# Spreading GpSimd's indirect transfers: permutation scatters three per tile, single-word lookups fewer per half tile

## What is computed

```python
def gat_conv(x, src, dst, W, a_src, a_dst, bias):
    h = (x @ W).reshape(n, H, C)                       # H, C = 4, 256
    al_s = jnp.einsum('nhc,hc->nh', h, a_src)
    al_d = jnp.einsum('nhc,hc->nh', h, a_dst)
    e = jax.nn.leaky_relu(al_s[src] + al_d[dst], NEG_SLOPE)
    w = jnp.exp(e - segment_max(e, dst)[dst])
    alpha = w / segment_sum(w, dst)[dst]
    return segment_sum(h[src] * alpha[:, :, None], dst).reshape(n, H * C) + bias
h = relu(gat_conv(x, src, dst, W1, a_src1, a_dst1, b1))
h = relu(gat_conv(h, src, dst, W2, a_src2, a_dst2, b2))
x = layernorm(x + h @ Wfc + bfc)     # then three more layers on the edges
```

## Time and profile before

| | |
|---|---|
| timed runs | 2668.86 us median of 3 (2668.79 to 2675.23) |
| the profiled execution | 2661.8 us; span 2659.9 us |
| TensorE | 2356.0 us busy, 89%; granted clock 0.934 of full on average |
| weight loads | 1885.9 us, 71% |
| VectorE | 1527.7 us, 57% |
| ScalarE | 995.7 us, 37% |
| GpSimd | 1001.7 us, 38% |
| DMA | mean 148 GB/s |

### The profile page before, as it was taken

One profiled execution on the slowest core, in us unless ns is written; L12 is line 12 of the kernel. 1 busy time (PEld: TensorE's weight loads), 2 busy tenths in 40 slices (PEclk: granted clock), 3 DMA queues, 4 the chain that ended last, 5 costly groups with the idle time before them and its releaser, 6 DMA issues.

```text
span 2659.9 us, 33436 instructions
## 1 busy us (share of the span) xinstructions
PE 2356.0 (89%) x10787; PEld 1885.9 (71%) x10787; DVE 1527.7 (57%) x4649; ACT 995.7 (37%) x2005; POOL 1001.7 (38%) x971
## 2 busy tenths in 40 slices
PE   6977593696999998888989999999998987999997
PEld 4856482485788886766877888888886766777775
DVE  6746371474466683333433566378776765667754
ACT  4932010121126651111212566334433553555343
POOL 1052517302512226553052322135664544543532
PEclk8988796798999998988999999999999999999998
DMA  5323251354236752222222667456665655555432
GB/s 177 138 90 111 66 185 45 99 178 142 75 120 232 250 205 84 64 65 71 96 66 74 228 216 251 139 188 214 204 203 190 230 183 179 165 180 184 160 109 68
DMA packets 171539, 394.21 MB, mean 148 GB/s; under 512 B 44967, under 2 KB 73902, under 8 KB 170830
## 3 DMA queue, kind: packets, MB, share of 16 engines
q0 software_dynamic: 65296, 184.67, 22.4%
q1 hardware_dynamic: 106090, 207.66, 22.2%
HBM read 221.98 MB, written 170.25 MB: 147 GB/s over the span
## 4 chain that ended last, share of the span: by engine, by line
PE 61%; DVE 5%; issue 5%; ACT 2%; another core or an unknown queue 2%; DMA 1%; POOL 0%; DVEq 0%; ACTq 0%; SPq 0%; POOLq 0%
PE g_h_ps L2440 11%; PE g_h_ps L2442 11%; PE g_h_ps L2441 11%; PE g_t_ps L2421 5%; PE g_h_ps L2467 4%; PE g_h_ps L2465 4%; PE g_h_ps L2466 4%; PE g_h_ps L1712 1%; PE g_h_ps L1710 1%; PE g_h_ps L1711 1%; DVE g_x_hi L2690 1%; PE g_sum_ps L962 1%; PE g_sum_ps L963 1%; PE g_t_ps L1696 1%
## 5 line engine op out<-in xcount | busy, mean ns | idle before, releaser
L2440 PE MATMUL g_h_ps<-held_w_hi,g_x_hi 128*128 128x512 f32 x1264 | 520.9, 412 | 17.3 <-issue 14.4
L2441 PE MATMUL g_h_ps<-held_w_lo,g_x_hi 128*128 128x512 f32 x1264 | 503.4, 398 | 19.3 <-issue 19.2
L2442 PE MATMUL g_h_ps<-held_w_hi,g_x_lo 128*128 128x512 f32 x1264 | 503.8, 399 | 17.6 <-issue 17.0
L2542 ACT ACTIVATE g_act_t<-g_t_ps,g_b_col 128x256 f32<-128x256 f32 (+1 forms) x640 | 263.7, 467 | 529.5 <-PE g_t_ps L2421 349.4
L591 DVE CUSTOM_DVE_ANT_0 g_prod<-g_h_sb,g_a_rows 128x256 f32<-128x256 f32 x632 | 224.7, 420 | 247.5 <-ACT g_h_sb L489 166.1
L2690 DVE CAST g_x_hi<-g_act_t 128x512 fp32r<-128x512 f32 (+1 forms) x320 | 154.6, 483 | 344.1 <-ACT g_act_t L2542 290.3
L420 PE MATMUL g_h_ps<-g_w_hi,g_x_hi 128*128 128x512 f32 x616 | 250.5, 407 | 94.8 <-issue 52.9
L2442 PEld LDWEIGHTS g_h_ps<-held_w_hi,g_x_lo 128*128 128x128 f32 x1264 | 242.9, 192 | 76.5 <-issue 23.6
L2441 PEld LDWEIGHTS g_h_ps<-held_w_lo,g_x_hi 128*128 128x128 f32 x1264 | 243.8, 193 | 69.3 <-issue 25.7
L2440 PEld LDWEIGHTS g_h_ps<-held_w_hi,g_x_hi 128*128 128x128 f32 x1264 | 243.0, 192 | 67.0 <-issue 19.9
L2465 PE MATMUL g_h_ps<-fc_w_hi,g_x_hi 128*128 128x512 f32 x632 | 280.2, 443 | 1.0 <-DVE g_x_lo L2692 0.7
(11 more groups left out here) (386 smaller groups left out, 4094.4 us busy)
## 6 DMA issues: line engine op xcount, KB each, us to landing
h<-g_h_sb SPq DMA_DIRECT2D x158, 512.0 KB
g_x_in<-h SPq DMA_DIRECT2D x59, 512.0 KB
g_x_in<-in_dram SPq DMA_DIRECT2D x40, 512.0 KB
h<-g_rows_own SPq DMA_DIRECT2D x40, 512.0 KB
x<-fc_x SPq DMA_DIRECT2D x20, 512.0 KB
x<-conv_x SPq DMA_DIRECT2D x20, 512.0 KB
g_w_raw<-in_dram SPq DMA_DIRECT2D x12, 512.0 KB, 4.7
fc_w_raw<-in_dram SPq DMA_DIRECT2D x20, 256.0 KB
```

Source lines behind the costliest of these rows:

```text
L2440: pe.matmul(out, xh, wh, start=(k == 0), stop=False)
L2441: pe.matmul(out, xh, wl, start=False, stop=False)
L2442: last = pe.matmul(out, xl, wh, start=False, stop=(k == KC - 1))
L2542: last = act.activation(act_t[:, k, 0:width], t_ps[f % 2][:, c, 0:width], ACT.Relu, bias=b_col[:, m // GM, k:k + 1])
```

## The change

The permutation's scatters wait for tiles: before each group of three stands a wait for one tile of the first stage more. In the second stage two lookups of slots, not four, stand at a half, and three lookups in the maps, not four; both take more halves, and `set_slots` with its wait moves ten halves later.

```diff
@@ dense_and_prep
+    PERM_FROM = 4 * (RANKED + 7)
@@ GpSimd's program of the first stage
                 for c in range(TILES):
+                    if c % 3 == 0:
+                        pool.wait_ge(tile_done, 4 + PERM_FROM + c // 3)
                     pool.indirect_dma_start(perm_tab, bass.IndirectOffsetOnAxis(slot_i[:, c:c + 1], 0),
                                             perm[:, c, :], None).then_inc(slots_out, 16)
@@ node_layers, GpSimd
-                def look_maps(t):
-                    ends = lambda k: bass.IndirectOffsetOnAxis(side[:, t, k:k + 1].bitcast(I32), 0)
-                    for n, (map_in, k) in enumerate(((map_d, P_DST), (map_d, P_SRC), (map_s, P_SRC), (map_s, P_DST))):
-                        pool.indirect_dma_start(found[:, t, n:n + 1], None, map_in, ends(k)).then_inc(looked, 16)
+                def look_map(n):
+                    t, n = divmod(n, 4)
+                    map_in, k = ((map_d, P_DST), (map_d, P_SRC), (map_s, P_SRC), (map_s, P_DST))[n]
+                    ends = bass.IndirectOffsetOnAxis(side[:, t, k:k + 1].bitcast(I32), 0)
+                    pool.indirect_dma_start(found[:, t, n:n + 1], None, map_in, ends).then_inc(looked, 16)
@@ the walk over h
-                    if SUMS1 + SPAN + 2 <= h < SUMS1 + SPAN + 12:
-                        k = h - (SUMS1 + SPAN + 2)
-                        look_slots(2 * k)
-                        look_slots(2 * k + 1)
-                    if h == SUMS1 + SPAN + 14:
+                    if SUMS1 + SPAN + 2 <= h < SUMS1 + SPAN + 2 + ET:
+                        look_slots(h - (SUMS1 + SPAN + 2))
+                    if h == SUMS1 + SPAN + 4 + ET:
                         pool.wait_ge(slots_set, 1)
-                    if SUMS1 + SPAN + 14 <= h < SUMS1 + SPAN + 34:
-                        look_maps(h - (SUMS1 + SPAN + 14))
+                    for n in range(3 * (h - (SUMS1 + SPAN + 4 + ET)), 3 * (h - (SUMS1 + SPAN + 3 + ET))):
+                        if 0 <= n < 4 * ET:
+                            look_map(n)
@@ VectorE
-                    if h == SUMS1 + SPAN + 13:
+                    if h == SUMS1 + SPAN + 3 + ET:
                         set_slots()
```

## The result

The changed kernel takes 2546.24 us (median of 4 runs, 2537.84 to 2555.53) beside 2668.82 us of the kernel before (4 runs): ratio 0.9556, 95% interval 0.952 to 0.9592. The profiled execution took 2555.53 us with a span of 2553.5 us, 106.4 us under that of before; TensorE is 2341.6 us busy (92%) and its clock 0.952 of full on average. The medians lie 122.6 us apart; the two traces account for 106.4 of them, since the profiled execution was the slowest of the four here, and before it was 7.0 us under its median.

The account below looks back on a forecast made before the run. TensorE bounds the kernel, so gains come from its holes under GpSimd's unbroken indirect-DMA rows. 2661.8 - 71 (first stage) - 39 (second stage) = 2551.8 us, plus 7.1 for the median: 2559 us; range 2518 to 2603.

Parts of the forecast that it names:

- pauses and short rows are wholly free: Rival, both stages: rows of 14 and the first 24 us row cost nothing, all 147 us come, 2522 us; chance 0.12.
- a row of 14 as dear as 18: Rival, second stage: a 14-DMA row costs as much as one of 18, gain 81 us, 2588 us; chance 0.12.
- 1.9 us are too short: Rival, first stage: pauses help only after some 2 us, TensorE loses 2 us per tile, 2603 us; chance 0.11.
- spacing makes no difference: Rival, first stage: each scatter has its price wherever it stands, so 2669 us; chance 0.02.
- slower: Rival, first stage: small gaps at each tile hold TensorE at 1.2 GHz, up to 2696 us; chance 0.03.
- Onset and end: GpSimd's DMA rows: TensorE's trouble begins 17 to 18 us after a row's start, ends 3.1 us after the row.
- pauses give back at least 3.1 to one: Spread scatters, first stage: each us of pause buys 3.1 us of row or more, so 1.9 us per tile suffices.
- The charge of 10 us for the catching up: First stage: a first row of some 18 scatters, 24 us, while GpSimd catches up, costs 10 us (bounds 0 and 30).
- not 71: First-stage term: the scatter row's 81 us come back less a charge of 10, so -71 us.
- The net term, 39 us: Second-stage term: the lookups' seven long rows cost 66 us, 27 stay, so -39 us.
- as forecast (4.5): Second stage: each of six rows of 14 costs 4.5 us, 2.2 idle and 2.3 at 1.2 GHz; 27 in all.
- one of 6, free: Second stage: the new lookups include one row of 6 DMAs that costs nothing, with GpSimd's `set_slots` wait still 6.25 us.

Follow-up runs that it names:

- experiment 1: Kernel before with only the scatters changed to three per tile, lookups as before, on the chip that does not starve: 2406.64 us, ratio 1.0006.
- experiment 2: Kernel before with only the lookups changed, scatters in one row as before, on the chip that does not starve: 2404.59 us, ratio 1.0006.
- experiment 3: Changed kernel plus a GpSimd wait for TensorE's progress at each half of the lookups, on the chip that does not starve: 2404.97 us, ratio 1.0006.
- experiment 4: Kernel before plus four GpSimd scratch fills ahead of every twelfth permutation scatter, on the chip that does not starve: 2406.88 us, ratio 1.0018.
- experiment 11: Changed kernel plus 79 direct GpSimd transfers in one row ahead of the wait for `slots_done`: 2542.32 us, ratio 0.9539 to the kernel before.
- experiment 8: Changed kernel with four scatters per tile in place of three: 2552.58 us, ratio 0.9587 to the kernel before.
- experiment 5: The changed kernel itself measured again, on a chip where the kernel before takes 2670.48 us: 2544.91 us, ratio 0.9508.
- experiment 6: Kernel before with only the scatters changed to three per tile, on a chip where the kernel before takes 2670.48 us: 2589.79 us, ratio 0.9684.
- experiment 7: Changed kernel plus a GpSimd wait for the half tile before each half's lookups, where the kernel before takes 2670.48 us: 2521.01 us, ratio 0.9451.
- experiment 9: Kernel before plus four GpSimd fills of a small tile ahead of every twelfth permutation scatter, where the kernel before takes 2663.22 us: 2583.04 us, ratio 0.9696.
- experiment 12: Changed kernel plus 79 indirect GpSimd transfers with 16-row lists in one row, where the kernel before takes 2667.07 us: 2630.77 us, ratio 0.9866.

## Why the prediction was right

**The time.** 2559 us was forecast and 2546 measured. Between the profiled executions the sum was closer, 2551.8 against 2555.53; that the median would lie 7.1 us above the profiled execution, as before, did not hold (it lies 9.3 below). Of the rivals, *pauses and short rows are wholly free* (2522) and *a row of 14 as dear as 18* (2588) lie 24 and 42 us off on either side; *1.9 us are too short* (2603) is refuted by the 65.00 of 65.00 busy us after; *spacing makes no difference* holds on the chip of experiments 1 to 4 and nowhere else; *slower* did not appear, as the clock stood at 1.00 of full under the spread scatters. The rule of the Trainium skill that was weighed ("DMA: Bandwidth & Descriptors", section "Issuing engines are not separate DMA queues": all engines' transfers share the same 16 DMA engines, so that issuing from several engines at once saves only issue time) speaks of who issues; that spacing should not matter either was my own step from it. That step fits the one chip that does not starve, with its ratios of 1.0006 and 1.0018, and the direct transfers of experiment 11; it fits no long unbroken row of indirect ones on the others.

**Onset and end.** They held where they were read. The first late matmuls in five rows of the second stage after start 17.1 to 19.2 us after the row's start. In the first stage 16 transfers and 22.1 us (385.0 to 407.1) passed without one; there TensorE's onset is nearer to the 24 us that the earlier trace rows already allowed. ScalarE's is not: its copy due at 404.65, 18.6 us after the first scatter, came 4.0 us late, and before, the copy due at 406.4 came at 417.96. The row of 28, with transfers of 4.28 and 1.78 us in it, shows its first late matmul after 29.8 us. So the time from the row's start alone is not the rule, as experiment 8 shows.

**The first stage.** The step "pauses give back at least 3.1 to one" was used below its range and held: 1.4 us are enough for three scatters. The 3.1 itself came from a row misread: it had begun at 677.17. If the 3.4 us that its transfers took beyond 0.95 us each count as a pause with the 2.13, my estimate from these rows is 3.1 again, so the number stands on that condition. Experiment 8 does not test the step, since its GpSimd hardly paused. The charge of 10 us for the catching up was mis-sized: it is 0, since only ScalarE was late and TensorE had another tile to work on. So 81.1 us came, not 71.

**The second stage.** The net term, 39 us, measured 38.0 between the two traces and 44.9 between the medians of experiments 5 and 6; the near hit is partly luck. Rows of 10 cost nothing and four rows of 14 cost 3.7, 4.4, 4.3 and 4.3 us, as forecast (4.5). But of these some 2.2 us are the stretch at the lower clock, and it does not always come. In experiment 5's trace the clock stood at 1.00 beside four rows of 14, and they cost 1.4 to 1.6 us each:

```profile
1141.04:1166.16 25.12, 23.87 (x113) 19.51 (x112) 9.80 (x41) 5.31 (x13) 13.98 (x14) 1.00 0.27 85
```

The step "one of 6, free" failed: GpSimd waited for `set_slots` until 1054.40 (18.76 us, not the 6.25 of the earlier trace rows), the six lookups lasted until the next gathers' condition was met, and they joined the next 14 to a row of 20, 11.6 us dear in place of 4.5. The last row of 14 cost 2.3, and 2.0 came back behind the others. Experiment 7 shows the cure.

**What I did not see.** I took work behind and ahead of the changed lines as fixed. The row of 28 at the score gathers cost some 9 us, by timing alone; it formed in the traces of the result and of experiments 5 and 6, and not in those of before and of experiments 7 to 9, 11 and 12. And I had no case for "the starvation itself may not be there": on one chip the whole gain is nothing.

**What stays open.** What the engines lack during a row is argued, not shown. It is not the transfer of their instructions as the page counts it: the two instruction queues show the same lines where the kernel starves and where it does not, here of experiment 2's kernel and, alike, of the changed one:

```profile
q8 instruction: 77, 1.26, 0.2%
q14 instruction: 76, 0.62, 0.1%
```

Nor is it known what makes a row harmless, a wait instruction within it or a transfer that takes longer (experiment 8); a row of 79 with a met wait ahead of every fourth transfer and nothing else changed would tell, and was not run.

And it is not known what sets the one chip apart. It was used once, so it may be a state of the chip at that time and not the chip.

## What to carry to other kernels

Where TensorE's gaps are put down to "issue" while GpSimd issues indirect transfers back to back, look at how long the row stands without a break, not at how much it moves. Long unbroken rows were dear and short ones free on the chips that starve, but one row of 45 us with met waits in it was free too, so read TensorE's holes before pricing a row. Break it before 15 us, with a wait for a tile or with GpSimd's own compute, and tie each group to progress, since rows that are apart in the code join when GpSimd runs late. Before pauses go into a row, see who waits for its end: where nobody does, all comes back (81 of 81 us); where VectorE does, about half was lost again (35.5 of 67.1 us came back). And measure on more than one chip before such a gain is believed.

## What the runs showed of the hardware

- GpSimd issuing indirect transfers without a pause keeps TensorE short from 17 to 19 (second stage, experiment 12) or 24 us (permutation of before) on, down to one matmul per 2.80 us, and ScalarE from 19 us on, in the first measurement and on two chips of the experiments; on one chip rows of 90 transfers and of 112 us cost nothing, with the same least issue time. The kernel of before takes 2663 to 2670 us on those and 2404 on this.
- Direct transfers of the same size (0.541 us each) starve nobody in 44 us; indirect ones with 16 entries (0.839 us and 0.30 between) starve like those with 128 (0.967 us).
- 4.56 us of GpSimd's own compute after 12 indirect transfers is a full pause.
- A row of 31 in 45 us, with a met wait ahead of every fourth and six transfers of 1.4 to 1.9 us, cost TensorE no "issue" wait (experiment 8), and 18 in 25.8 us, with two of 3.25 and 1.77 us, none either (kernel of before).
- Under a row an engine that waits for a finished tile can go on late though TensorE had no hole: ScalarE 4.0 us late at 408.66, GpSimd 0.25 us after it (result's trace).
